# Eight probability tiles, one mixing per batch element, reciprocals in the bank of the mixed values, and a new order on every queue

## The chip, the cores and the metric
The kernel runs on one core of a Trainium2 chip. The metric is the device time of one execution in microseconds, the median of several runs. TensorE is called PE, VectorE the vector engine or DVE, ScalarE ACT, GpSimd POOL and SyncE SP, as in the profile.

## What is computed
A batch of 64 sequences of 128 tokens with 256 channels goes through two blocks of attention and feed-forward, each on a layer-normalised input with a residual added:

```python
x = x + L0_xattn(_layernorm(x), ctx, ctx, mask, ...)   # 16 heads of 16 channels, biases
x = x + L0_ffn(_layernorm(x), W1, b1, W2, b2)          # ternary weights, 1024 hidden, relu
x = x + L1_xattn(_layernorm(x), ctx, ctx, lens, ...)   # keys beyond lens masked
x = x + L1_ffn(_layernorm(x), ...)                     # 8 autoencoders, the best one's adapter
```

Both attentions are `softmax(q k^T / 4) v` per head and take keys and values from the same context. The last layer computes for each sequence the reconstruction error of eight small autoencoders, picks the best, and adds a base matmul and that expert's adapter.

## The kernel before
**Pairs and slots.** The batch is cut into 32 pairs of sequences (`NP`, `PB` = 2, so `T` = 256 tokens). One loop `for t in range(FIRST, END)` is written out for each engine. `at(t, o)` yields pair p where `t = 16 p + o`, so a step with offset o runs for pair p in slot 16 p + o, and offsets 0 to 77 mean that up to five pairs are in work at once. Within a slot the order is that of the text. A slot is no unit of time: it only fixes the order of instructions on each engine's own queue. Across engines everything is ordered by semaphores (`Signal`).

**Attention of one layer l for a pair.** `scores(l, p, j)`, j = 0 to 7 (four for each sequence b), puts four heads' scores of 128 x 128 into the bank `S`; `maximum(l, p, j)` on the vector engine takes the row maxima (layer 0 adds the mask's bias, line 863; layer 1, line 855). After four of them `split_max(l, p, b)` splits the 16 maxima of each token into two half-precision parts and turns them into rows (`mrows`, lines 870 to 877). SP's `maxima(l, p, b)` copies these rows with four transfers into `qs`, as two more rows of the contraction. `scores_t(l, p, j)` then computes the transposed scores with the maximum already taken off into the bank `X`, `exps` on ACT turns them into a tile of `pT`, and in layer 0 POOL's `apply_mask` multiplies the tile by the mask. `mix(l, p, u)` multiplies two such tiles with the values into half of the bank `V`: 8 matmuls with 32 columns of weights each, four side by side in the array. Half of a head's 32 columns of weights hold ones, so that the softmax's denominator comes with the values. `turn_out(l, p, b)` transposes `V` in 32 x 32 blocks to `otok`, `scale_out(l, p, b)` takes the reciprocals (`rden`), multiplies (`atok`) and transposes to `attT`, and `output(l, p)` projects. `add_att` adds the result, `statistics` computes the moments of the next layer norm.

**Keys and queries.** `keys` and `queries` leave their result in a bank; `high` (ACT) and `low` (vector engine) split it into two half-precision parts in `packed`; SP's `spill(l, j, p)` (j = 1 keys, 0 queries) writes that to DRAM and `stack(l, j, p)` reads it back head by head with four transfers (and one for the mask's row of the keys). `scores(l, p, 0)` waits for all nine transfers of the two stacks.

**The last layer.** `hidden`, `reconstruct(p, m)` (experts 2m and 2m + 1, row groups of 64), `differences(p, e)` on the vector engine, `squares` on ACT, `losses`, `choose`, SP's `gather` of the chosen adapter (two transfers of 192.5 KB), `down`, `up`, `add_up`, `store`.

**Banks.** `S`, `X` and `V` are one bank each; all other results share five banks dealt out in `BANKS`. `claim` makes PE wait until the former holder of a bank has been read. `exps(l, p, j)` writes tile `j % 4` of four and waits for the mixing that read it.

**SP's order** within a period: `maxima(1, 1)`, `load`, `stack(1, 1)`, `spill(1, 0)`, `maxima(0, 0)`, `stack(1, 0)`, `gather`, `spill(0, 1)`, `maxima(0, 1)`, `stack(0, 1)`, `spill(0, 0)`, `maxima(1, 0)`, `stack(0, 0)`, `store`, `spill(1, 1)`.

Of the kernel before, what the change touches and what calls it, by code (L numbers as in the profile page):

```python
# [8 lines left out]
F32 = mybir.dt.float32  # L9
# [13 lines left out]
H = 16  # L23
# [10 lines left out]
UNITS = 2 * PB  # L34
# [13 lines left out]
def pair16(value):  # L48
# [14 lines left out]
END = BODY * (NP - 1) + 77  # L63
# [34 lines left out]
def build(nc, x, lens, mask, mask_t, wq0, bq0, wk0, bk0, wv0, bv0, wo0, bo0, w1t, b1, w2t, b2,  # L98
          wq1, wk1, wv1, wo1, w_base, wd1, bd1, wd2, bd2, adapters, ctx_in, out):
    with ExitStack() as ctx:  # L100
# [118 lines left out]
        mix_ready = [signal(f"mix_ready{l}", UNITS) for l in range(2)]  # L219
# [101 lines left out]
        def _(sp):  # L321
# [84 lines left out]
            for t in range(FIRST, END):  # L406
                for p in at(t, 48):
                    maxima(1, p, 1)
                for p in at(t, -14):
                    load(p)  # L410
                for p in at(t, 34):
                    stack(1, 1, p)
                    spill(1, 0, p)
                for p in at(t, 4):
                    maxima(0, p, 0)
                for p in at(t, 36):
                    stack(1, 0, p)
                for p in at(t, 71):
                    gather(p)
                for p in at(t, -7):  # L420
                    spill(0, 1, p)
                for p in at(t, 10):
                    maxima(0, p, 1)
                for p in at(t, -6):
                    stack(0, 1, p)
                for p in at(t, -5):
                    spill(0, 0, p)
                for p in at(t, 44):
                    maxima(1, p, 0)
                for p in at(t, -4):  # L430
                    stack(0, 0, p)
                for p in at(t, 76):
                    store(p)
                for p in at(t, 29):
                    spill(1, 1, p)
# [9 lines left out]
        def _(pool):  # L445
# [73 lines left out]
            def apply_mask(p, j):  # L519
                exp_done[0].done(pool, p, j)  # L520
                keep_ready.done(pool, p)
                blk = pT[:, j % 4].rearrange("p (a t) -> p a t", a=4)
# [8 lines left out]
            for t in range(FIRST, END):  # L531
                for p in at(t, 16):
                    normalise(1, p, 0)
                for p in at(t, 19):
                    normalise(1, p, 1)
                for p in at(t, -11):
                    mask_parts(p)
                    rstd_of(0, p)
                for p in at(t, -10):
                    normalise(0, p, 0)  # L540
                    normalise(0, p, 1)
                for p in at(t, 6):
                    apply_mask(p, 0)
                for p in at(t, 7):
                    apply_mask(p, 1)
                for p in at(t, 23):
                    h_lows(p, 0)
                for p in at(t, -8):
                    mask_bias(p)
                for p in at(t, 8):  # L550
                    apply_mask(p, 2)
                for p in at(t, 24):
                    h_lows(p, 1)
                for p in at(t, 9):
                    apply_mask(p, 3)
                for p in at(t, 26):
                    add_bias(1, p)
                for p in at(t, -6):
                    add_bias(0, p)
                for p in at(t, 26):  # L560
                    h_lows(p, 2)
                    h_lows(p, 3)
                for p in at(t, 10):
                    apply_mask(p, 4)
                for p in at(t, 58):
                    rstd_of(3, p)
# [3 lines left out]
                for p in at(t, 11):  # L570
                    apply_mask(p, 5)
                for p in at(t, 12):
                    apply_mask(p, 6)
                for p in at(t, 13):
                    apply_mask(p, 7)
                for p in at(t, 29):
                    rstd_of(2, p)
                    normalise(2, p, 0)
                for p in at(t, 30):
                    normalise(2, p, 1)  # L580
                for p in at(t, 15):
                    rstd_of(1, p)
# [7 lines left out]
        def _(act):  # L590
# [32 lines left out]
            def exps(l, p, j):  # L623
                st_ready[l].done(act, p, j)
                if j >= 4:
# [842 lines left out]
```

## Time and profile before
| | |
|---|---|
| median of 3 runs | 1717.36 us (1717.09 to 1728.58) |
| the profiled execution | 1727.22 us, span 1725.2 us |
| mean granted TensorE clock | 0.969 of full speed |
| PE busy | 1584.5 us, 92%, 15136 matmuls |
| vector engine busy | 1316.8 us, 76% |
| ACT busy | 891.8 us, 52% |
| POOL busy | 1104.2 us, 64% |
| DMA | 157.24 MB, 91 GB/s |

The span runs from the first to the last instruction of one execution; the rest of its time lies around it. Busy time is the union of an engine's instructions; a PE matmul's length contains the tail of its pipeline, so the distance from one start to the next is the better measure of what a block costs. An idle time is listed with the event that ended it. The chain that ended last goes back from the last instruction to what released each step.

### The profile page before, as it was taken

To read this page: it belongs to the slowest core of one execution; us is meant where nothing else is said; L and a number is where in the kernel's file an instruction comes from. 1 tells how busy PE (TensorE), PEld (TensorE's weight loads), DVE (VectorE), ACT (ScalarE), POOL (GpSimd) and SP (SyncE) were. 2 spreads that over 40 slices of the span, in tenths; PEclk is the share of its full clock that TensorE was granted. 3 is DMA by queue.
4 is the path that set the end of the run, shared out by engine and by line. 5 is a ranking of instruction groups with operands and counts; after the bars stand their busy time and mean duration, and the time that the engine had idled before them with its cause. 6 is when DMAs were issued, how large, how long until landed. Compare 5 with 4: busy or idle time off the path is not lost.

```text
span 1725.2 us, 44058 instructions
## 1 busy us (share of the span) xinstructions
PE 1584.5 (92%) x15136; PEld 1279.1 (74%) x15136; DVE 1316.8 (76%) x5086; ACT 891.8 (52%) x2465; POOL 1104.2 (64%) x1198
## 2 busy tenths in 40 slices
PE   2578999999999999999999999999999999999776
PEld 1356777778878887778887877788788877877554
DVE  6446788888887888888887888888788888886542
ACT  0134455655555556555555556555555565555432
POOL 4467776666676776666667766666677766655200
PEclk9789999999999999999999999999999999999976
DMA  7445555555555454555555545555555555552300
GB/s 187 81 74 92 87 88 92 96 103 97 97 95 108 83 96 96 103 97 94 97 103 94 94 90 98 101 95 99 97 106 82 97 97 102 97 77 54 57 18 26
DMA packets 286213, 157.24 MB, mean 91 GB/s; under 512 B 38820, under 2 KB 281640, under 8 KB 285992
## 3 DMA queue, kind: packets, MB, share of 16 engines
q1 hardware_dynamic: 285992, 154.44, 49.6%
q8 instruction: 121, 1.98, 0.6%
q14 instruction: 100, 0.82, 0.2%
HBM read 111.36 MB, written 41.96 MB: 89 GB/s over the span
## 4 chain that ended last, share of the span: by engine, by line
PE 47%; DVE 38%; issue 7%; DMA 3%; POOL 2%; ACT 1%; SPq 1%; DVEq 0%; ACTq 0%; POOLq 0%
DVE dump L863 11%; PE psD L1239 7%; PE psD L1228 7%; DVE dif L929 6%; PE psD L1207 4%; PE psD L1153 4%; PE psD L1273 4%; PE psS L1168 3%; PE psD L1142 3%; PE psV L1195 3%; PE psX L1180 3%; DVE atok L894 3%; PE psD L1249 3%; DVE otok L886 2%; DVE m L872 2%
## 5 line engine op out<-in xcount | busy, mean ns | idle before, releaser
L633 ACT ACTIVATE pT<-psX 128x512 f32<-128x512 f32 x512 | 305.9, 597 | 351.7 <-PE psX L1180 351.6
L523 POOL TENSOR_TENSOR pT<-pT,keep 128x512 f32<-128x512 f32 x256 | 323.1, 1268 | 108.2 <-ACT pT L633 105.6
L508 POOL TENSOR_SCALAR xn<-xr,mv,rstd 128x256 f32<-128x256 f32 x256 | 311.5, 1224 | 13.7
L855 DVE TENSOR_REDUCE mx<-psS 128x4 f32<-128x512 f32 x256 | 175.7, 686 | 170.8 <-PE psS L1168 168.4
L482 POOL TENSOR_SCALAR veps<-mv 128x2 f32<-128x2 f32 x128 | 29.5, 230 | 392.3 <-DVE mv L808 389.6
L929 DVE SCALAR_TENSOR_TENSOR dif<-psD,bd2s,xT 128x256 f32<-128x256 f32 x512 | 216.8, 472 | 63.6 <-PE psD L1249 63.5
L863 DVE CUSTOM_DVE_ANT_0 dump<-psS,bias 128x128 bf16<-128x128 f32 x1024 | 232.5, 282 | 30.8 <-PE psS L1168 30.7
L1168 PE MATMUL psS<-ks,qs 65*128 65x128 f16 x2048 | 202.6, 221 | 49.2 <-DVE mx L863 22.6
L677 ACT ACTIVATE dif<-dif 128x256 f32<-128x256 f32 x512 | 207.4, 412 | 25.8 <-DVE dif L929 24.7
L1180 PE MATMUL psX<-qs,ks 67*128 67x128 f16 x2048 | 200.4, 220 | 15.5 <-ACT pT L633 8.7
L1168 PEld LDWEIGHTS psS<-ks,qs 65*128 65x128 f16 x2048 | 141.6, 98 | 97.8 <-issue 34.0
L1180 PEld LDWEIGHTS psX<-qs,ks 67*128 67x128 f16 x2048 | 141.6, 98 | 55.6 <-issue 18.6
L1195 PE MATMUL psV<-pT,v 128*32 128x128 f32 x4096 | 165.9, 280 | 8.0 <-POOL pT L523 4.3
L528 POOL TENSOR_TENSOR hhl<-work,hhl 128x512 f16<-128x512 f32 x128 | 151.5, 1193 | 11.9 <-ACT hhl L663 11.9
L1207 PE MATMUL psD<-wo,attT 128*128 128x256 f32 x512 | 132.1, 403 | 19.3 <-DVE attT L898 19.2
L1249 PE MATMUL psD<-hd,wd2s 64*128 64x256 f32 x1024 | 146.3, 405 | 2.0 <-DVE dif L929 2.0
L1195 PEld LDWEIGHTS psV<-pT,v 128*32 128x32 f32 x4096 | 96.8, 109 | 61.4 <-issue 39.3
L1220 PE MATMUL psD<-xs,w1q 128*128 128x256 f16 x1024 | 134.0, 274 | 1.4 <-DVE xs L911 0.8
L1142 PE MATMUL psD<-xT,wq 128*128 128x256 f32 x512 | 132.0, 394 | 1.5 <-DVE keep L822 1.5
L1153 PE MATMUL psD<-wv,ctxT 128*128 128x256 f32 x512 | 130.5, 399 | 0.0
L606 ACT ACTIVATE xT<-psD 128x512 f32<-128x512 f32 x96 | 57.1, 595 | 137.4 <-PE psD L1113 137.4
L1239 PE MATMUL psD<-xT,wd1s 128*128 128x256 f32 x512 | 126.0, 390 | 0.7 <-ACT xT L606 0.7
(103 smaller groups left out, 3125.3 us busy)
## 6 DMA issues: line engine op xcount, KB each, us to landing
scr<-packed SPq DMA_DIRECT2D x128, 256.0 KB, 2.3
ks<-scr SPq DMA_DIRECT2D x256, 128.0 KB, 4.5
qs<-scr SPq DMA_DIRECT2D x256, 128.0 KB, 4.4
adapter<-in_adapters SPq DMA_DIRECT2D x64, 192.5 KB, 2.5
xr<-in_x SPq DMA_DIRECT2D x32, 256.0 KB, 2.8
ctxT<-in_ctx SPq DMA_DIRECT2D x32, 256.0 KB, 2.8
qs<-mrows SPq DMA_DIRECT2D x512, 2.0 KB
out_y<-xr SPq DMA_DIRECT2D x32, 256.0 KB, 4.9
```

The costliest lines, as they stand in the source:

```text
L508: nc.gpsimd.tensor_scalar(xn[:, XN[s], b], xr[:, p % NX, b], mv[:, s, b, 0:1], rstd[:, s, b:b + 1], ALU.subtract, ALU.mult).then_inc(norme ...
L523: nc.gpsimd.tensor_tensor(blk, blk, keep[:, p % 2, j // 4].unsqueeze(1).to_broadcast([P, 4, P]), ALU.mult).then_inc(masked.sem, 1)
L633: nc.scalar.activation(pT[:, j % 4], X[:], ACT.Exp, scale=SCALE).then_inc(exp_done[l].sem, 1)
L677: nc.scalar.activation(blk, blk, ACT.Square, accum_out=acc[:, e, b:b + 1]).then_inc(squared.sem, 1)
L863: ins = nc.vector.tensor_tensor_reduce(out=dump[:, a], in0=S[:, a * P:a * P + P], in1=bias0[:, p % 2, b], scale=1.0, scalar=-3e38, op0=ALU ...
L929: nc.vector.scalar_tensor_tensor(out=dif[:, e % 4, k], in0=bank[f"rec{e}"][:, k * T:k * T + T], scalar=bd2s[:, e, k:k + 1], in1=xT3[:, p % ...
L1153: ins = nc.tensor.matmul(dst[:, b * D:b * D + D], ctxT[:, p % NC, k * T + b * P:k * T + b * P + P], wv[l][:, k], start=(k == 0), stop=(k = ...
L1168: ins = nc.tensor.matmul(S[:, a * P:a * P + P], qs[0:MASK_ROW + 1, r, h, t0:t0 + P], ks[0:MASK_ROW + 1, r, h, t0:t0 + P], start=True, stop ...
L1180: ins = nc.tensor.matmul(X[:, a * P:a * P + P], ks[0:ROWS, r, h, t0:t0 + P], qs[0:ROWS, r, h, t0:t0 + P], start=True, stop=True)
L1195: ins = nc.tensor.matmul(V[32 * a:32 * a + 32, (2 * half + s) * P:(2 * half + s) * P + P], v2[l][:, b, half * UH + 2 * a + s], pT[:, (2 * ...
L1207: ins = nc.tensor.matmul(dst[:, b * D:b * D + D], attT[:, l, b, k], wo[l][:, k], start=(k == 0), stop=(k == KD - 1))
L1239: ins = nc.tensor.matmul(dst[:, m * T:m * T + T], wd1s[:, k, e0:e0 + 2].rearrange("p e r -> p (e r)"), xT3[:, p % 2, k], start=(k == 0), s ...
```

## The change
`pT` has eight tiles instead of four, so that `exps` writes tile j and waits only for the other layer's mixing of a neighbouring pair. `mix(l, p, b)` does all four tiles of a sequence in one go and signals once. It claims `V` after `normalised` (the multiplication) instead of `turned`, since the reciprocals now lie in `V[:, 0:H]` and no longer in `rden`. The five banks are dealt anew. And every queue has a new order. The sum of the work is the same.

```diff
-    ("cnt", "rec5", "v1", "hd0", "q0"),
-    ("v0", "q1", "T2", "F1_1", "T0", "hd1", "T3"),
-    ("O0", "F1_2", "rec1", "loss", "rec7", "up"),
-    ("O1", "k0", "rec6", "rec3", "F2", "down", "rec0"),
-    ("rec2", "F1_0", "T1", "k1", "F1_3", "rec4"),
+    ("F1_0", "q1", "O0", "F1_3", "T0", "rec1", "F1_1", "hd0", "up"),
+    ("v0", "rec4", "rec3", "k1", "hd1", "down", "T3"),
+    ("loss", "rec7", "rec0", "F1_2"),
+    ("k0", "rec6", "T2", "v1", "O1"),
+    ("rec2", "cnt", "T1", "rec5", "F2", "q0"),
...
-        pT = sb("pT", [P, 4, 512], F32)
+        pT = sb("pT", [P, QUADS, 512], F32)
-        rden = sb("rden", [P, 2, H], F32)
...
             def exps(l, p, j):
                 st_ready[l].done(act, p, j)
-                if j >= 4:
-                    mix_ready[l].done(act, p, (j - 4) // 2)
-                elif l:
-                    mix_ready[0].done(act, min(p + 2, NP - 1), 2 + j // 2)
-                    mix_ready[1].done(act, p - 1, 2 + j // 2)
+                if l:
+                    mix_ready[0].done(act, min(p + 2, NP - 1), j // 4)
                 else:
-                    mix_ready[1].done(act, p - 3, 2 + j // 2)
-                    mix_ready[0].done(act, p - 1, 2 + j // 2)
-                nc.scalar.activation(pT[:, j % 4], X[:], ACT.Exp, scale=SCALE).then_inc(exp_done[l].sem, 1)
+                    mix_ready[1].done(act, p - 3, j // 4)
+                nc.scalar.activation(pT[:, j], X[:], ACT.Exp, scale=SCALE).then_inc(exp_done[l].sem, 1)
...
             def turn_out(l, p, b):
-                mix_ready[l].done(dve, p, 2 * b + 1)
+                mix_ready[l].done(dve, p, b)
...
-                nc.vector.reciprocal(rden[:, l], otok[:, l, :, HD]).then_inc(recip_done[l].sem, 1)
+                nc.vector.reciprocal(V[:, 0:H], otok[:, l, :, HD]).then_inc(recip_done[l].sem, 1)
                 recip_done[l].done(dve, p, b)
-                nc.vector.tensor_tensor(atok[:, l], otok[:, l, :, 0:HD], rden[:, l].unsqueeze(2).to_broadcast([P, H, HD]),
+                nc.vector.tensor_tensor(atok[:, l], otok[:, l, :, 0:HD], V[:, 0:H].unsqueeze(2).to_broadcast([P, H, HD]),
...
-            def mix(l, p, u):
-                b, half = u // 2, u % 2
-                if half == 0:
-                    claim("V", turned[l], p, b)
-                if u == 0:
+            def mix(l, p, b):
+                claim("V", normalised[l], p, b)
+                if b == 0:
...
-                (exp_done[1] if l else masked).done(pe, p, 2 * u + 1)
-                for s in range(2):
+                (exp_done[1] if l else masked).done(pe, p, 4 * b + 3)
+                for n in range(4):
                     for a in range(4):
...
```

The new orders, cut to the period of 16 slots as they follow one another in the loop. Numbers in brackets are the slot within the period; steps of different pairs stand side by side.

SP: [2] `store`, [3] `maxima(1, 1)`, [5] `load`, [6] `spill(1, 0)`, [7] `maxima(0, 0)`, `stack(1, 0)`, [8] `gather`, [9] `maxima(0, 1)`, [10] `spill(0, 1)`, [12] `spill(1, 1)`, `stack(0, 1)`, [13] `spill(0, 0)`, `maxima(1, 0)`, `stack(0, 0)`, `stack(1, 1)`.

PE: [0] `reconstruct(1)`, `scores(0, 0)`, `scores_t(1, 2)`, [1] `values(1)`, `scores(0, 1)`, `scores_t(1, 3)`, `output(0)`, `turn(2)`, [2] `scores(0, 2)`, `mix(1, 0)`, `scores_t(1, 4)`, `reconstruct(2)`, [3] `scores_t(1, 5)`, `scores(0, 3)`, [4] `queries(1)`, `reconstruct(3)`, `scores(0, 4)`, `turn(1)`, `scores_t(1, 6)`, [5] `values(0)`, `scores_t(1, 7)`, `scores(0, 5)`, `keys(0)`, `count`, [6] `ffn_up(0)`, `losses`, `scores(0, 6)`, `scores_t(0, 0)`, `mix(1, 1)`, [7] `scores(0, 7)`, `scores_t(0, 1)`, [8] `ffn_up(1)`, `keys(1)`, `scores_t(0, 2)`, `turn(0)`, `scores(1, 0)`, [9] `ffn_up(2)`, `scores_t(0, 3)`, `scores(1, 1)`, [10] `ffn_up(3)`, `output(1)`, `scores_t(0, 4)`, `scores(1, 2)`, [11] `queries(0)`, `scores_t(0, 5)`, `scores(1, 3)`, [12] `down`, `scores_t(0, 6)`, `scores(1, 4)`, `mix(0, 0)`, `up`, [13] `scores_t(0, 7)`, `scores(1, 5)`, `ffn_down(0)`, `turn(3)`, [14] `ffn_down(1)`, `scores(1, 6)`, `hidden(0)`, `hidden(1)`, `scores_t(1, 0)`, [15] `scores(1, 7)`, `reconstruct(0)`, `scores_t(1, 1)`, `mix(0, 1)`.

The vector engine's first half, old: [0] `differences(1)`, `maximum(0, 0)`, `scale_out(0, 1)`, [1] `differences(2)`, `maximum(0, 1)`, `differences(3)`, `add_att(0)`, [2] `maximum(0, 2)`, `statistics(1)`, `turn_out(1, 0)`, [3] `maximum(0, 3)`, `differences(4)`, `differences(5)`, [4] **`split_max(0, 0)`**, `low(1, 0)`, `statistics(0)`, `differences(6)`, `maximum(0, 4)`, `any_of`, [5] `differences(7)`, `x_lows`, and so on. New: [0] `differences(1)`, `split_max(1, 1)`, `turn_out(0, 1)`, `maximum(0, 0)`, [1] `scale_out(0, 1)`, `differences(2)`, `maximum(0, 1)`, `differences(3)`, [2] `add_att(0)`, `maximum(0, 2)`, `statistics(1)`, `turn_out(1, 0)`, [3] `differences(4)`, `differences(5)`, `maximum(0, 3)`, `statistics(0)`, [4] `low(1, 0)`, `maximum(0, 4)`, `differences(6)`, `any_of`, **`split_max(0, 0)`**, `differences(7)`, `x_lows`, [5] `maximum(0, 5)`, [6] `scale_out(1, 0)`, `maximum(0, 6)`, `choose`, `values0`, and so on; the period ends in both with [15] `maximum(1, 7)` and `differences(0)`, which in the old order had `statistics(2)`, `split_max(1, 1)` and `turn_out(0, 1)` around them.

On POOL the layer norm's steps and `add_bias` move by up to four slots among the eight `apply_mask`; on ACT `squares`, `values1`, the `high` and `h_highs` steps move by one or two.

## Rows read from the trace of the kernel before
**Rows 1.** The stage table: window, us, busy times (instructions), clock, DMA share, GB/s.
```profile
400.00:600.00 200.00, 195.93 (x1922) 160.10 (x1922) 163.82 (x641) 112.43 (x312) 140.53 (x154) 1.00 0.55 98
```

**Rows 2.** The page: PE's busy tenths in 40 slices.
```profile
PE   2578999999999999999999999999999999999776
```

**Rows 3.** PE's waits, 400 to 1400 us: total, times, longest.
```profile
PE psD L1207 <- DVE attT L898: 10.2, 20, 0.5
PE psS L1168 <- DVE mx L863: 8.2, 20, 0.5
```

**Rows 4.** The chain that ended last, in order of time: start, us, what.
```profile
848.46 0.29 DVE dump L863
...
873.91 0.46 DVE attT L898
...
897.40 0.29 DVE dump L863
```

**Rows 5.** PE's timeline: start, us, line, output and input, shapes, count.
```profile
853.44 0.65 PE L1195 MATMUL psV<-pT,v 128*32 128x128 f32 x16
854.01 1.14 PE L1249 MATMUL psD<-hd,wd2s 64*128 64x256 f32 x8
...
870.12 0.39 PE L1168 MATMUL psS<-ks,qs 65*128 65x128 f16 x4
...
893.51 1.14 PE L1249 MATMUL psD<-hd,wd2s 64*128 64x256 f32 x8
894.57 0.65 PE L1195 MATMUL psV<-pT,v 128*32 128x128 f32 x16
...
896.98 0.39 PE L1168 MATMUL psS<-ks,qs 65*128 65x128 f16 x4
897.20 0.39 PE L1180 MATMUL psX<-qs,ks 67*128 67x128 f16 x4
897.52 0.70 PE L1249 MATMUL psD<-hd,wd2s 64*128 64x256 f32 x4
```

**Rows 6.** The mixing's line, weight loads: ns min/median/max, first and last start.
```profile
L1195 PEld LDWEIGHTS psV<-pT,v x2624: 106/110/110, 405.1 to 1397.1; 128*32 128x32 f32 x188
```

**Rows 7.** The vector engine's timeline, columns as in rows 5.
```profile
856.61 1.66 DVE L929 SCALAR_TENSOR_TENSOR dif<-psD,bd2s,xT 128x256 f32<-128x256 f32 x4
858.18 0.17 DVE L870 TENSOR_SCALAR m<-mx 128x16 f16<-128x16 f32 x1
...
858.72 0.65 DVE L837 TENSOR_TENSOR packed<-psD,packed 128x512 f16<-128x512 f32 x1
...
862.11 0.87 DVE L929 SCALAR_TENSOR_TENSOR dif<-psD,bd2s,xT 128x256 f32<-128x256 f32 x2
...
867.67 0.75 DVE L886 STREAM_TRANSPOSE otok<-psV 128x256 f32<-128x256 f32 x2
...
869.57 1.08 DVE L872 SCALAR_TENSOR_TENSOR m<-mx,m 128x16 f16<-128x16 f32 x1
```

**Rows 8.** SP's timeline: start and length of issues, their count.
```profile
886.25 3.31 SPq L361 DMA_DIRECT2D qs<-scr  x4
...
957.74 2.61 SPq L377 DMA_DIRECT2D qs<-mrows  x4
960.39 1.88 SPq L361 DMA_DIRECT2D qs<-scr  x4
```

**Rows 9.** The tile `qs`, 961.7 to 962.4 us: its stack's last transfers.
```profile
DMA to landing us min/median/max: 4.8/4.9/5.1
```

**Rows 10.** Two lines of the vector engine: ns min/median/max.
```profile
L894 DVE TENSOR_TENSOR atok<-otok,rden x81: 424/425/830, 409.1 to 1387.9; 128x256 f32<-128x256 f32 x81
...
L845 DVE TENSOR_TENSOR v<-psD,bvb x40: 411/417/424, 423.8 to 1354.1; 128x256 f32<-128x256 f32 x40
```

**Rows 11.** POOL's timeline, columns as in rows 5.
```profile
869.47 1.15 POOL L528 TENSOR_TENSOR hhl<-work,hhl 128x512 f16<-128x512 f32 x1
```

More of the change, by code:

```diff
@@ L693, in _ @@
                 for p in at(t, 49):
+                    values1(p)
                     exps(1, p, 3)
@@ L729, in _ @@
                     h_highs(p, 0)
+                for p in at(t, -9):
+                    high(0, 1, p)
+                for p in at(t, 23):
                     relus(p, 1)
+                for p in at(t, 8):
+                    exps(0, p, 2)
+                for p in at(t, -8):
+                    copy_xT(0, p)
                 for p in at(t, 24):
                     high(1, 1, p)
-                for p in at(t, 8):
-                    exps(0, p, 2)
                 for p in at(t, 25):
@@ L974, in _ @@
                     differences(p, 1)
+                for p in at(t, 48):
+                    split_max(1, p, 1)
+                for p in at(t, 16):
+                    turn_out(0, p, 1)
                 for p in at(t, 0):
                     maximum(0, p, 0)
-                for p in at(t, 16):
+                for p in at(t, 17):
                     scale_out(0, p, 1)
@@ L992, in _ @@
                     turn_out(1, p, 0)
-                for p in at(t, 3):
-                    maximum(0, p, 3)
                 for p in at(t, 67):
@@ L997, in _ @@
                     differences(p, 5)
+                for p in at(t, 3):
+                    maximum(0, p, 3)
+                for p in at(t, -13):
+                    statistics(0, p)
+                for p in at(t, 36):
+                    low(1, 0, p)
+                for p in at(t, 4):
+                    maximum(0, p, 4)
+                for p in at(t, 68):
+                    differences(p, 6)
+                for p in at(t, -12):
+                    any_of(p)
                 for p in at(t, 4):
                     split_max(0, p, 0)
[L1000 to L1003 removed]
                 for p in at(t, 68):
[L1005 to L1010 removed]
                     differences(p, 7)
[L1012 removed]
+                for p in at(t, 20):
                     x_lows(p)
@@ L1023, in _ @@
                     choose(p)
-                for p in at(t, 54):
-                    turn_out(1, p, 1)
+                for p in at(t, 6):
+                    values0(p)
                 for p in at(t, 7):
@@ L1069, in _ @@
                     maximum(1, p, 7)
-                    split_max(1, p, 1)
                 for p in at(t, 63):
                     differences(p, 0)
-                for p in at(t, 15):
-                    turn_out(0, p, 1)
                 if t == GAMMA_SLOT:
@@ L1282, in _ @@
             for t in range(FIRST, END):
-                for p in at(t, 48):
-                    values(1, p)
+                for p in at(t, 64):
+                    reconstruct(p, 1)
                 for p in at(t, 0):
@@ L1327, in _ @@
                     scores_t(1, p, 7)
-                for p in at(t, -11):
-                    count(p)
                 for p in at(t, 5):
@@ L1333, in _ @@
                     keys(0, p)
+                    count(p)
                 for p in at(t, 22):
                     ffn_up(p, 0)
+                for p in at(t, 70):
+                    losses(p)
                 for p in at(t, 6):
@@ L1350, in _ @@
                     scores_t(0, p, 2)
+                for p in at(t, -8):
+                    turn(0, p)
                 for p in at(t, 40):
@@ L1379, in _ @@
                     scores(1, p, 3)
-                for p in at(t, 75):
-                    up(p)
+                for p in at(t, 76):
+                    down(p)
+                for p in at(t, 12):
+                    scores_t(0, p, 6)
                 for p in at(t, 44):
```

258 lines of the change are left out of this document (115 added, 143 removed).

## The prediction

> **What bounds the kernel now.** I read the stage table first, then PE's waits, the chain of waits, and last the timelines of one period. In the loop PE is busy 195.93 of 200 us, the vector engine 163.82, ACT 112.43, POOL 140.53, at a granted clock of 1.00 [rows 1]. About 28 periods of a pair run so: the slices with a 9 for PE [rows 2] are some 1,380 us. A period is 48.94 us (the chain's row at 848.46 comes back at 897.40). Only 1 us a period is idle: 10.2 us before the output projection in 20 periods and 8.2 us before `scores` [rows 3]. An idle time begins when the last matmul's 0.39 us are over, though the next could have followed after 0.22 (the row at 896.98 [rows 5]), so 0.17 is lost ahead of each: 0.51 + 0.17 and 0.41 + 0.17, 1.26 us in all.
>
> The chain says where the period is made. From the first maximum (848.46) to the transposed `attT` (873.91) it runs without a break on the vector engine, then on PE to the next `scores(0, p, 0)` [rows 4]. So the first half is bound by the vector queue in order, the second by PE. Work put into the first vector half lengthens the period, unless something there has slack.
>
> I count from R, the end of `reconstruct(p, 0)`: 893.51 + 1.06 = 894.57 [rows 5], one period earlier 845.63. Layer 1's `scores(1, p, 0)` starts at 870.12, R + 24.49, and from there PE needs 24.45 us to the next R.
>
> **What PE saves.** A mixing unit starts at 853.44 and the next block at 854.01: 0.57 us. It has four rounds of four column groups, and a round's weight loads take 110 ns each [rows 6]; if rounds follow at that spacing they are 0.44, and 0.13 is paid once per unit (between 0 and that; I take it whole, since 0.57 is not a multiple of the spacing), and 8 units become 4: 4 x 0.13 = 0.53 us. Before a unit or a `reconstruct`, the full-array block in front takes 0.10 more: 896.98 to 897.20 is 0.22 for a score block, 897.20 to 897.52 is 0.32 [rows 5]. There are 8 such entries in the old order, 7 in the new one: 0.10. PE's work is thus 0.63 lighter. Without the 1.26 of waiting a period would be 48.94 - 1.26 - 0.63 = 47.05 us. (The Trainium skill, TensorEngine Tiling (Array Packing), Key Properties, says that changing the tiling mode drains the engine; by it alone each of the five boundaries that go would pay, and the rows agree with 0.10 to 0.13 at each.)
>
> **What the vector engine pays.** The new order puts five steps ahead of `split_max(0, p, 0)` that followed it: `low(1, 0)`, `statistics(0)`, `differences(6)`, `maximum(0, p, 4)`, `any_of`. They are one unbroken stretch in the old trace: 858.72 to 862.11, 3.39 us [rows 7]. What stood ahead of it stays: 848.46 to 858.18, 9.72 us. The split itself is 858.72 - 858.18 = 0.54, and its last instruction ends some 0.08 after the next one's start: 0.62. From the first maximum, M, the rows of layer 0 are now ready at M + 9.72 + 3.39 + 0.62 = M + 13.73.
> M: the old one was R + 2.83, set by `scores(0, p, 0)`. Now the queue in front is four difference instructions (856.61 to 858.18, 1.57), `split_max(1, p, 1)`, 0.54, and `turn_out(0, p, 1)`, 0.75 less the overlap of some 0.07 [rows 7], from R + 0.12: M = R + 2.91. PE reaches its score block at 0.33 of `scores_t` + mixing 1.01 + `reconstruct` 1.06 = R + 2.40 as before, so neither waits for the other. Rows ready: R + 16.64.
>
> **Where that goes: SyncE.** SP's queue is in order: spill of the queries of layer 1 (its low part is ready at about R + 14.2, well ahead), `maxima(0, p, 0)`, then `stack(1, 0, p)`. The stack cannot be issued before the maxima, and the maxima not before the rows. Issue of the four row transfers takes 957.74 to 960.39, 2.65 us, and the stack's last transfer is issued at 960.39 + 1.88 - 0.45 = 961.82 and lands 5.1 later: 6.5 us from the stack's first issue to its last landing [rows 8, 9]. So the stack lands at R + 16.64 + 0.1 + 2.65 + 6.5 = R + 25.9, and `scores(1, p, 0)` starts at R + 26.0. In the old order it came at 24.49 with no row of waiting.
> PE would be there earlier. Its blocks from R to this one were 24.49 less the wait of 0.58; new among them are `scores_t(1, p, 1)` 0.23, `turn(0)` 0.44, one unit more in fewer pieces, 0.57 - 3 x 0.13 = 0.18, and one entry 0.10: 24.86. So 1.1 us of waiting is in it. A part of it may be spent earlier, at `scores_t(0, p, 0)`, which wants the same rows in `qs` at R + 19.8 when their last transfer is issued at about R + 18.7; no row gives their landing, and up to 1.1 it costs nothing extra.
> After it PE has less left than before: 24.45, less three units and their entries (3 x 0.57 + 3 x 0.10), less `scores_t(1, p, 1)` 0.23 and `turn(0)` 0.44 which moved ahead, less the old wait 0.68, less 0.05 of a slower transpose behind a unit, plus one merged mixing and its entry, 1.11: 22.15. Period: 26.0 + 22.15 = **48.15**, and I take 48.2 for small waits that such a sum overlooks (ACT's exponential 5 behind `high(0, 0)`, and the bank of `turn(0)` freed by `relus` at nearly the moment it is wanted).
>
> **The rest of the change.** Eight tiles for the probabilities take away waits of ACT for a mixing; `exps` waits for `scores_t` in the old profile, so that is worth 0. The price is that a mixing waits for four masks: POOL ends mask 3 some 2 us ahead of PE. Hidden by that slack. Held `V`: the bank is now free after the multiplication, not after the transpose, under 1 us later, and each mixing comes at least that much after `scale_out`: 0.
> Reciprocals in PSUM: `atok` takes 424 ns mostly and 830 at worst [rows 10]; the long one starts while POOL works on a two-input instruction. The same is seen at 869.57, where an instruction of 16 elements took 1.08 us (one of 858.18 took 0.17), to the end of POOL's 869.47 + 1.15 [rows 7, 11]. With one operand in PSUM I expect no holds: 0.4 of 4 x 0.45 us a period, but at `scale_out(1, 1)`, which no longer sets PE's time. A vector instruction of 256 elements with a PSUM operand takes 417 ns [rows 10], so 0 for the place, between -0.4 and +0.1.
> (Here a rule speaks against: the Trainium skill, VectorE: DVE Perf Modes, section on the TRN2 errata, gives PSUM sources 62 cycles more than SBUF ones; by it the one `scale_out` on the chain would add under 0.1 us a period. The rows, 417 against 424, do not show it.)
> Banks are dealt anew: I followed each claim; the closest, `count` behind `x_lows`, costs under 0.1. The stores move behind five slots in SP's order, past `gather` and `load`, which are issued long before their data is wanted.
>
> **The sum.** 48.94 - 48.2 = 0.74 us a period x 28 = 21 us. Filling and draining the loop I charge with 1 us more, for mixings that wait for four tiles. The profiled execution: 1725.2 - 20 = 1705 of span. It was 1727.22 us where the median of the runs is 1717.36, so the forecast is 1717.4 - 20 = **1697 us**.
>
> **Rivals.**
> *A, the stack is not late.* Then PE alone bounds: 47.05, say 47.1. 28 x 1.84 = 52 us: 1666. For it: PE idles only 1 us now. Against: six terms from rows make the chain 1.1 us longer than PE's blocks ahead of it. Chance 0.10.
> *B, no change.* The chain is a little longer than I add up: the stack's issue can stall (886.25 took 3.31 us for four such transfers [rows 8], 1.4 more than 960.39), or a short vector instruction is held 0.9 us behind POOL as at 869.57, now in the split of layer 0. A stall or a hold adds 0.5 to 0.9: 48.7 to 49.1, 1711 to 1722. POOL has no two-input mask work at that time, which speaks against the hold. Chance 0.30.
> *C, slower: `gather` shares the DMA engines with the late stack.* SP can issue it once `choose` is done on the vector engine, by the same counting at R + 21.6, so in the middle of the stack's flight; the old order had it as the stack landed. If they divide the engines' time, up to 2.5 us come on top: period 50.7, + 1.76 x 28 = 49 us: 1767. It decides from 1.35 us on (slower by 1%). For it: the engines carry other traffic in half of the time already (DMA share 0.55 [rows 1]). Against: the transfers are on one queue, the stack's first, and its issue is over at about R + 21.4. Chance 0.17, with other new waits of that size.
> *The forecast*: chance 0.43, by itself 1685 to 1708.
>
> About 1% is what a measurement of this kernel can tell from no change. Faster by over 1% (below 1700): A and most of the forecast, 0.47. Within 1%: the rest of the forecast and B, 0.34. Slower: 0.19 (C and a little of B). Range: 1668 to 1735, which leaves out half of A and two thirds of C.
>
> **What would show it.** Right: a period near 48.2; a wait of PE of about 1 us at `scores(1, p, 0)` for the transfer into `qs`, perhaps one at `scores_t(0, p, 0)` for the rows, none before the output projection; merged mixings of 1.01 us; `atok` never over 450 ns. Wrong: no DMA among PE's waits (A); a stack landing 8 us or more after its issue (C); waits of PE for POOL's masks or for the vector engine's `scale_out`, which would mean that the slack of the merged mixing was misread.

## The result

| | changed kernel | kernel before |
|---|---|---|
| median of the runs, same chip | 1709.21 us (1706.53 to 1712.03, 7 runs) | 1719.5 us (1717.09 to 1728.58, 7 runs) |
| ratio | 0.992, 95% interval 0.9899 to 0.9941 | |
| profiled execution | 1706.53 us | 1727.22 us |
| its span | 1704.7 us | 1725.2 us |

Faster by 0.8%. The forecast of the span was 1705 us, that of the time 1697. The measured 1709.21 lies in the stated range, and 1 us above the 1685 to 1708 that the forecast gave for its own case. Span and time differ so much because the sum was made against the profiled execution, and taken off the median. The profiled execution of before lay 8 us above the median of its runs, that of the changed kernel 3 us below. The same instructions in the same order were timed once more on another chip (the run with the gather later, below): 1710.51 us against 1724.23, ratio 0.9918.

### The profile after

The stage table of the loop's first stretch, which answers to [rows 1] (columns as there):

```profile
400.00:600.00 200.00, 194.98 (x1967) 162.13 (x1965) 159.63 (x653) 118.15 (x321) 138.62 (x150) 1.00 0.60 97
```

PE is no busier than before. Its waits between 400 and 1400 us, which answer to [rows 3] (columns: waited for; us in total, times, longest us):

```profile
PE psS L1165 <- DMA qs<-scr: 13.8, 21, 1.1
PE psX L1177 <- DMA qs<-mrows: 10.2, 21, 0.6
```

The two old waits are gone: none before the output projection, next to none for `mx`. In their place stand two for SP's transfers, in every period: at `scores_t(0, p, 0)` for the rows of maxima, and at `scores(1, p, 0)` for the stack of layer 1. One period on PE (start, duration, what is computed, and in brackets the wait ahead of it); R, the end of `reconstruct(p, 0)`, is 838.40, where `scores_t(1, p, 1)` begins, and the last row is the next one's:

```profile
838.40 0.40 PE L1177 MATMUL psX<-qs,ks 67*128 67x128 f16 x4
838.73 1.08 PE L1190 MATMUL psV<-pT,v 128*32 128x128 f32 x32
839.74 1.13 PE L1244 MATMUL psD<-hd,wd2s 64*128 64x256 f32 x8
...
858.83 0.38 PE L1177 MATMUL psX<-qs,ks 67*128 67x128 f16 x4 [0.46 <-DMA qs<-mrows]
...
864.88 0.38 PE L1165 MATMUL psS<-ks,qs 65*128 65x128 f16 x4 [0.78 <-DMA qs<-scr]
...
866.20 0.39 PE L1165 MATMUL psS<-ks,qs 65*128 65x128 f16 x4
...
886.89 0.40 PE L1177 MATMUL psX<-qs,ks 67*128 67x128 f16 x4
```

A merged mixing takes 839.74 - 838.73 = 1.01 us, `scores(1, p, 0)` begins at R + 26.48, and the next R is 22.01 later (886.89). Over 22 periods the two are 26.36 and 22.06 on average: 48.42 us. (In all that follows, places in a period are averages over the 21 to 23 periods that begin between 400 and 1450 us, unless one is shown.) The same chain on the vector engine and on SP (SP's rows: start of the first issue, time of issuing, transfers):

```profile
851.86 0.66 DVE L832 TENSOR_TENSOR packed<-psD,packed 128x512 f16<-128x512 f32 x1
...
854.06 0.41 DVE L809 TENSOR_REDUCE allc<-mqf 128x2 f32<-128x256 f32 x1
854.38 0.17 DVE L865 TENSOR_SCALAR m<-mx 128x16 f16<-128x16 f32 x1
854.59 0.18 DVE L867 SCALAR_TENSOR_TENSOR m<-mx,m 128x16 f16<-128x16 f32 x1
854.80 0.21 DVE L872 STREAM_TRANSPOSE mrows<-m 128x32 f16<-128x32 f16 x1
...
855.04 2.59 SPq L375 DMA_DIRECT2D qs<-mrows  x4
857.67 1.88 SPq L359 DMA_DIRECT2D qs<-scr  x4
860.97 1.53 SPq L383 DMA_DIRECT2D adapter<-in_adapters  x2
```

Rows ready at 855.01, R + 16.6; stack issued from 857.67, R + 19.3; landed when PE goes on, 7.2 us later (7.09 on average: 6.95 to the last landing, and then the start of the block). The period, from one `add_up` to the next, is 48.95 us before (26 intervals, all within 0.1) and 48.37 after (47.6 to 49.0: it moves with the landings). Of the 20.5 us between the spans, 14.9 are these 26 intervals, 0.6 came before the first, and 5.0 lie in the last five.

**What else is gone.** The old order had two more losses on the vector engine, in each of 22 periods, and both stood on the chain that ended in the projection of `attT`. The split of layer 0's second batch, `split_max(0, p, 1)`, was held for 0.9 us behind POOL ([rows 7] has one, at 869.57), and the multiplication ahead of that projection took 0.64 to 0.83 us instead of 0.42:

```profile
873.05 0.82 DVE L894 TENSOR_TENSOR atok<-otok,rden 128x256 f32<-128x256 f32 x1
```

In the changed kernel the first is held in 3 of 22 periods and the second in none. What the old kernel would gain if only these two were taken away was not tried.

### The profile page after: what moved, and what is told of

The parts are those of the page before. It is cut to its first block, busy times and chain, and to the rows that moved or that the text cites. A ratio compares the mean times of both kernels' runs of the same rounds, so it can differ in the third digit from the quotient of the medians.

```text
span 1704.7 us, 43831 instructions
## 1 busy us (share of the span) xinstructions
PE 1554.4 (91%) x15136; PEld 1282.7 (75%) x15136; DVE 1271.5 (75%) x5086; ACT 912.5 (54%) x2465; POOL 1098.4 (64%) x1198
## 4 chain that ended last, share of the span: by engine, by line
PE 45%; DVE 24%; DMA 12%; issue 9%; SPq 7%; POOL 2%; ACT 1%; POOLq 0%; DVEq 0%; ACTq 0%
DMA qs<-scr 10%; DVE dif L924 7%; DVE dump L858 7%; PE psD L1234 6%; PE psD L1223 6%; SPq L375 4%; PE psS L1165 4%; PE psD L1202 4%; PE psD L1139 4%; PE psD L1268 3%; PE psD L1215 3%; PE psX L1177 3%; PE psD L1244 3%; SPq L359 2%; PE psV L1190 2%
## 5 line engine op out<-in xcount | busy, mean ns | idle before, releaser
L522 POOL TENSOR_TENSOR pT<-pT,keep 128x512 f32<-128x512 f32 x256 | 318.6, 1271 | 5.5 <-ACT pT L629 5.5
L1165 PEld LDWEIGHTS psS<-ks,qs 65*128 65x128 f16 x2048 | 136.8, 98 | 114.9 <-issue 70.6
L653 ACT ACTIVATE work<-psD,b1s 128x256 f32<-128x256 f32 x256 | 107.8, 475 | 71.2 <-PE psD L1215 60.1
L1190 PE MATMUL psV<-pT,v 128*32 128x128 f32 x4096 | 140.1, 278 | 5.2 <-POOL pT L522 3.4
L1127 PE MATMUL psD<-ctxT,wk 128*128 128x256 f32 x512 | 124.6, 387 | 13.3 <-DVE bqr L961 13.3
L1223 PE MATMUL psD<-w2q,hhl 128*128 128x256 f16 x1024 | 122.0, 273 | 0.5 <-POOL hhl L527 0.5
```

Of the source, the lines that this page charges most:

```text
L522: nc.gpsimd.tensor_tensor(blk, blk, keep[:, p % 2, j // 4].unsqueeze(1).to_broadcast([P, 4, P]), ALU.mult).then_inc(masked.sem, 1)
L1165: ins = nc.tensor.matmul(S[:, a * P:a * P + P], qs[0:MASK_ROW + 1, r, h, t0:t0 + P], ks[0:MASK_ROW + 1, r, h, t0:t0 + P], start=True, stop ...
L1223: ins = nc.tensor.matmul(dst[:, b * D:b * D + D], hhl[:, n % 2, n // 2, b * P:b * P + P], w2q[:, n // 2], start=(n == 0), stop=(n == 2 * K ...
```

## The experiments

The ratios are to the kernel before on the same chip. "Period" is the mean of the same 26 intervals, and the changed kernel's is 48.37.

### The chain, from both sides

**The split early, in the changed kernel.** `split_max(0, p, 0)` goes ahead of the five steps:

```
                 for p in at(t, 3):
                     maximum(0, p, 3)
+                    split_max(0, p, 0)
...
-                for p in at(t, 4):
-                    split_max(0, p, 0)
```

> The changed kernel with split_max(0, p, 0) moved on the vector engine from behind any_of to right behind maximum(0, p, 3), where the old order had it in effect; nothing else. My theory: the rows of layer 0 come about 3.4 us earlier, SP can issue them as soon as the spill of layer 1's queries is out (about R + 15.2 instead of R + 16.6), the stack lands near R + 24.9 and PE hardly waits for it: period 47.4 instead of 48.4 us, in all about 25 us less than the changed kernel, 1683 us, and PE's waits for the transfers into qs nearly gone. Rival (PE's work alone made the gain, the transfer waits are only where its slack happens to fall): the waits move elsewhere, less than 5 us of difference.

Measured: 1757.67 us, ratio 1.0182 (1.0165 to 1.0199), period 50.41. The transfers are hardly waited for any more, as the chain says: `scores(1, p, 0)` starts at R + 24.91 in most periods, where the forecast had PE ready at R + 24.86. But the kernel lost 2%. Its waits of PE:

```profile
PE psS L1164 <- DVE mx L850: 36.3, 20, 2.0
PE psS L1164 <- DMA qs<-scr: 2.0, 3, 1.0
```

and what stands behind the first of them, vector engine and POOL, then PE:

```profile
839.03 0.62 DVE L865 TENSOR_SCALAR m<-mx 128x16 f16<-128x16 f32 x1
839.68 1.20 DVE L867 SCALAR_TENSOR_TENSOR m<-mx,m 128x16 f16<-128x16 f32 x1
...
838.46 1.16 POOL L527 TENSOR_TENSOR hhl<-work,hhl 128x512 f16<-128x512 f32 x1 [0.23 <-ACT hhl L659]
839.58 1.27 POOL L514 TENSOR_TENSOR xr<-xr,bob 128x512 f32<-128x512 f32 x1
...
843.86 0.40 PE L1164 MATMUL psS<-ks,qs 65*128 65x128 f16 x4 [1.66 <-DVE mx L850]
...
845.05 3.42 PE L1201 MATMUL psD<-wo,attT 128*128 128x256 f32 x8
```

The other split, that of the second batch, now falls among POOL's two-input instructions. Its two instructions of 16 elements end with POOL's (839.65 with 839.62, 840.88 with 840.85) and take 1.82 us instead of 0.35 (2.2 in most periods). PE waits 1.66 us at `scores(1, p, 1)`, and then its granted clock falls. The table of that run has, for the 5 us before and the 3.4 us behind,

```profile
840.00:845.00 5.00, 3.34 (x37) 2.79 (x35) 4.90 (x13) 3.91 (x8) 4.85 (x5) 1.00 0.24 68
845.40:848.80 3.40, 3.40 (x13) 2.56 (x12) 0.97 (x3) 0.61 (x2) 2.76 (x3) 0.50 0.76 187
```

0.50 is the lower of the two levels, 1.2 instead of 2.4 GHz, so the output projection takes 3.42 us instead of 1.95. All 21 periods between 400 and 1450 us have the hold, but only 15 of them the lower clock. The length of the one wait doesn't tell which: behind a longer one the clock stayed, behind a shorter one, in another period, it fell:

```profile
894.76 0.40 PE L1164 MATMUL psS<-ks,qs 65*128 65x128 f16 x4 [1.99 <-DVE mx L850]
895.00:900.00 5.00, 5.00 (x36) 4.17 (x34) 3.99 (x10) 1.44 (x3) 3.89 (x4) 1.00 0.70 167
...
1193.34 0.45 PE L1164 MATMUL psS<-ks,qs 65*128 65x128 f16 x4 [1.09 <-DVE mx L850]
1193.60:1197.00 3.40, 3.40 (x16) 2.56 (x14) 1.92 (x4) 1.66 (x4) 3.40 (x3) 0.50 0.55 162
```

The 6 periods at full clock last 49.22 us, the 15 others 50.82. The hold alone thus costs 1.7 us a period against the 47.55 of the run below that has the early split without it, and the clock 1.6 more where it falls.

**The split late, in the kernel before**, behind `any_of`:

```
-                for p in at(t, 4):
-                    split_max(0, p, 0)
...
                 for p in at(t, -12):
                     any_of(p)
+                for p in at(t, 4):
+                    split_max(0, p, 0)
```

> The kernel before, with only split_max(0, p, 0) moved behind any_of on the vector engine, as the changed order has it. Theory of the chain: the rows come 3.4 us later, the stack of layer 1's queries lands at about R + 25.9, PE waits 1.5 us for it at scores(1, p, 0) and in exchange no longer for attT (0.7): period 49.7 instead of 48.94, about 21 us slower than before, 1740 us. Rival (PE and the vector engine bound the kernel, the transfers are hidden): within 3 us of the kernel before.

Measured: 1751.78 us, ratio 1.0143 (1.0122 to 1.0165), period 50.11. PE's waits show the two transfers of the changed kernel, and none for `attT`:

```profile
PE psS L1168 <- DMA qs<-scr: 26.4, 20, 1.9
PE psX L1180 <- DMA qs<-mrows: 14.8, 20, 0.9
```

So the wait for the stack follows the place of this one step, in either kernel. It is the price that the new slots pay. The period is 0.4 us longer than was expected, and the trace has the 0.4 in the stack's flight: it is issued from R + 19.3, as in the changed kernel, and `scores(1, p, 0)` starts at R + 26.3, 7.0 us later, where 25.9 was expected. From there to the next R it is 23.7, as expected.

### The two other parts

**Reciprocals in SBUF.**

```
+        rden = sb("rden", [P, 2, H], F32)
...
-                nc.vector.reciprocal(V[:, 0:H], otok[:, l, :, HD])...
-                nc.vector.tensor_tensor(atok[:, l], otok[:, l, :, 0:HD], V[:, 0:H].unsqueeze(2)...
+                nc.vector.reciprocal(rden[:, l], otok[:, l, :, HD])...
+                nc.vector.tensor_tensor(atok[:, l], otok[:, l, :, 0:HD], rden[:, l].unsqueeze(2)...
```

> The changed kernel with the reciprocals back in SBUF (rden), all else as changed. Theory of the holds: atok takes up to 0.83 us again when POOL has a two-input instruction in work, and one of the four in a period (scale_out(1, 1)) stands right ahead of the output projection of layer 1, where PE has no slack: about 0.3 us a period, 9 us in all, 1718 us. Rival (the place of 16 numbers does not matter, as I took it in the sum): 0, within 2 us of the changed kernel. By the rule on PSUM sources it would be faster by 1 to 2 us.

Measured: 1724.5 us, ratio 0.9993 (0.998 to 1.0005), period 49.02: 0.65 more, twice what was expected. The group of the multiplication in this kernel and in the changed one, 400 to 1400 us (busy us, mean ns | idle before):

```profile
L890 DVE TENSOR_TENSOR atok<-otok,rden 128x256 f32<-128x256 f32 x81 | 47.7, 589 | 2.8
```

```profile
L889 DVE TENSOR_TENSOR atok<-otok,psV 128x256 f32<-128x256 f32 x83 | 34.9, 421 | 2.9
```

and the place in this kernel's timeline where it matters (POOL, vector engine, PE):

```profile
872.82 2.49 POOL L523 TENSOR_TENSOR pT<-pT,keep 128x512 f32<-128x512 f32 x2
...
874.57 1.02 DVE L890 TENSOR_TENSOR atok<-otok,rden 128x256 f32<-128x256 f32 x1
...
876.22 1.97 PE L1203 MATMUL psD<-wo,attT 128*128 128x256 f32 x8 [0.37 <-DVE attT L894]
```

With both inputs in SBUF it is held behind POOL's two-input masks, in `scale_out(1, p, 1)`, and PE waits for it at `output(1, p)`, 5.4 us in 13 periods between 400 and 1400 us. From `scores(1, p, 0)` to the next R a period takes 22.51 us instead of 22.06, so 0.45 of the 0.65 can be put down to this place. The rest lies ahead of it, where the stack's landing varies, and no cause is shown. With one input in PSUM no instance is held. In the changed kernel `attT` is done at 867.10 and the projection begins at 867.30: a slack of 0.20.

**Mixings in halves**, each with its own entry, one score block apart (shown for one of the four):

```
+                for p in at(t, 50):
+                    mix(1, p, 0, 0)
                 for p in at(t, 2):
                     scores(0, p, 2)
                 for p in at(t, 50):
-                    mix(1, p, 0)
+                    mix(1, p, 0, 1)
```

> The changed kernel with each mixing issued in two halves again, with the score block that stood in front of it between them; still one signal, and V and the tiles as changed. PE's work grows by 4 x (0.13 + 0.10) = 0.9 us a period. Theory (the period is set by the chain over SP, whose wait absorbs what PE does ahead of it): three of the four mixings lie ahead of scores(1, p, 0) in a stretch with about 1.1 us of waiting, so only mix(0, 0) counts: 0.25 a period, about 7 us in all, 1716 us, and the wait for the stack shrinks by 0.7. Rival (PE bound): 0.9 a period, 26 us, 1735 us.

Measured: 1742.58 us, ratio 1.0095 (1.0073 to 1.0117), period 49.54, above both numbers. One split mixing:

```profile
844.37 0.39 PE L1177 MATMUL psX<-qs,ks 67*128 67x128 f16 x4
844.69 0.64 PE L1191 MATMUL psV<-pT,v 128*32 128x128 f32 x16
845.27 0.40 PE L1165 MATMUL psS<-ks,qs 65*128 65x128 f16 x4
845.59 0.65 PE L1191 MATMUL psV<-pT,v 128*32 128x128 f32 x16
846.17 1.13 PE L1270 MATMUL psD<-wb,xT 128*128 128x256 f32 x4
```

Two halves of 0.58 and two entries of 0.10 are 1.36, where the merged one has 1.01 + 0.10: 0.25 each, 1.0 us a period, near the 0.92 of the terms. The expectations went wrong on what a chain does with it. After `scores(1, p, 0)`, where PE bounds, 0.24 of it shows in most periods (22.24 against 22.00), the one mixing that stands there, and 0.37 on average (22.43 against 22.06). Ahead of it half a mixing now stands before `scores(0, p, 2)`, which the vector queue waits for in order (11.1 us in 20 periods, none in the changed kernel): that score block comes at R + 8.1 instead of R + 7.3, the rows at R + 17.4 instead of 16.6, and `scores(1, p, 0)` at R + 27.17 instead of 26.36. Of these 0.8 us, 0.14 come from the split mixing at R, and some 0.65 from the half that this edit puts ahead of the block, with its entry, where the merged mixing stands behind it. So the run prices this way of halving. It doesn't show that merging as such shortens the vector chain.

### Toward a version without the waits

**Three runs that were not what they were meant to be.** In this kernel the slots decide the order: a step of slot `o` is placed by `o` modulo 16, and the place in the text only orders steps of one slot. In the next three runs the edit on POOL (twice) and the one on SP moved text, and not slots.

```
 (POOL, with the split early as above)
-                    mask_bias(p)
                     normalise(0, p, 0)
...
                 for p in at(t, -9):
                     add_bias(0, p)
+                for p in at(t, -11):
+                    mask_bias(p)
+                for p in at(t, 22):
+                    h_lows(p, 0)
```

> The changed kernel with split_max(0, p, 0) right behind maximum(0, p, 3), as in the run with the early split, and with one more edit on POOL: mask_bias (two one-input instructions, 1.54 us) moves from ahead of normalise(0, p, 0) to behind add_bias(0, p), and h_lows(p, 0) behind it. The two-input add_bias(0) is then over about 1.1 us before split_max(0, p, 1), and h_lows(0) begins about when it ends, so only the one-input instruction is in flight. If the early split lost its gain to that hold (theory): split_max(0, p, 1) takes 0.54 us again instead of 1.9, no wait of 1.7 to 2.0 us at scores(1, p, 1), no fall of the clock, no DMA among PE's longer waits: period 47.3 to 47.7, 28 x 0.9 = 25 us under the changed kernel, ratio to before 0.977, about 1685. If the early split makes the vector queue itself too late for scores(1, p, 1) (rival): period 48.4 or more, ratio 0.992 or more.

As built, `mask_bias` moved behind `normalise(0, p, 0)` only, and `h_lows(p, 0)` stayed ahead of `add_bias(0, p)`. Measured: 1756.36 us, ratio 1.0205 (1.0177 to 1.0233), as the early split alone, with 35.8 us of waits for `mx` in 20 periods against 36.3. It says nothing on the theory.

> The changed kernel with split_max(0, p, 0) two steps earlier only (ahead of differences(6) and any_of, 1.11 us of vector work), and the same POOL edit as the run before it. The chain to the stack of layer 1 is 1.11 us shorter: the waits for the rows at scores_t(0, p, 0) (0.46 in the profile) and for the stack at scores(1, p, 0) (0.78) leave about 0.1 together: period 48.43 - 1.0 = 47.4 to 47.6, ratio 0.978, about 1687. Rival, the landing times set the rest and spread: a wait of 0.3 to 0.5 stays and the period is 47.9, ratio 0.985.

The split is moved as told (ahead of `differences(6)`), the POOL edit is the same ineffective one. Measured: 1747.08 us, ratio 1.0141 (1.011 to 1.0173), waits for `mx` 33.1 us, for the transfers 2.3. So even 1.1 us of an earlier split brings the collision: what shields the second split in the changed kernel is PE's wait of 0.46 us at `scores_t(0, p, 0)`, which delays POOL's `h_lows` behind it: the second split starts at R + 23.2 in the changed kernel and in this one, and POOL's instruction at R + 23.6 there and R + 23.0 here. (The lower clock follows in 10 of 21 periods; these last 50.8 us, nearly all others 49.2.) And the shield is thin. In the changed kernel's own trace POOL's instruction starts at 862.01, 0.02 after the split's second one ends, and 3 of 22 periods show the hold (at 813.52, 1.06 us instead of 0.18).

> The changed kernel with gather(p) behind maxima(0, p, 1) in the order of SP, so that the 2 adapters are not on the queue while the stack of layer 1 is in flight. Theory (no sharing worth speaking of): the stack lands as before, 7 us behind its first issue, period within 0.1 of 48.43, ratio 0.992. Rival (the adapters share the engines with the stack): it lands 0.5 us or more earlier, PE's waits for it fall by 10 us of 21 in 20 periods, period 47.9, ratio 0.983. Slower by up to 0.3 a period if the queue of SP, 1.5 us later behind it, makes a spill late.

Here SP's order came out unchanged, so this is the changed kernel timed again: 1710.51 us, ratio 0.9918 (0.9892 to 0.9944), period 48.43.

The kernel before was profiled once more as well.

> The kernel before once more, for a second profile: the profiled execution shown was 1727.22 us where the median is 1717.36. If the 10 us lie in the loop, its period is 48.6 here against 48.94 there; if they lie at the start or the end, the period is 48.94 again and the first add_up comes earlier than 248.1 us, or the last one's tail is shorter.

Measured: 1727.68 us, period 48.94 again; the first `add_up` at 251.3 us (248.1 in the other), the last five intervals 198.5 us (201.1). In both the loop is the same and the ends differ by 3 us, in opposite directions. Both profiled executions lie at the upper end of this kernel's runs (1717 to 1729), so where the 10 us down to its median lie stays open.

**The POOL edit in slots that work.**

```
                 for p in at(t, -11):
-                    mask_bias(p)
                     normalise(0, p, 0)
...
                 for p in at(t, 22):
                     add_bias(1, p)
-                    h_lows(p, 0)
                 for p in at(t, -9):
                     add_bias(0, p)
+                    mask_bias(p)
+                for p in at(t, 23):
+                    h_lows(p, 0)
```

> The edit that the two runs before were meant to have, now in the slots that put it there: on POOL, add_bias(0, p) directly behind add_bias(1, p), then mask_bias(p) (one input, 1.54 us), then h_lows(p, 0); with split_max(0, p, 0) behind maximum(0, p, 3) as in the run with the early split. Counted from R of that run: add_bias(0) ends at R + 22.4, mask_bias fills R + 22.4 to 23.9, and split_max(0, p, 1) runs at R + 23.56 to 24.1. Theory (the hold by POOL's two-input instructions ate the gain of the early split): no hold, scores(1, p, 0) at R + 25.2, the vector queue lets scores(1, p, 1) start at R + 26.9, from there 20.7 to the next R as in the changed kernel: period 47.6, 28 x 0.8 = 23 us under the changed kernel, ratio 0.979, about 1687. Rival (the vector queue is late there even without a hold, or the hold only moves): period 48.4 or more, ratio 0.992 or more.

Measured: **1680.93 us** (1676.78 to 1684.1), ratio 0.9733 (0.9713 to 0.9753), period 47.55: faster than both kernels. POOL, then the vector engine, in the period whose R is 829.39:

```profile
850.47 1.28 POOL L514 TENSOR_TENSOR xr<-xr,bob 128x512 f32<-128x512 f32 x1
851.85 1.52 POOL L475 TENSOR_SCALAR bias<-mqf,allc 128x128 f32<-128x128 f32 x2
853.45 1.17 POOL L527 TENSOR_TENSOR hhl<-work,hhl 128x512 f16<-128x512 f32 x1
...
852.60 0.17 DVE L866 TENSOR_SCALAR m<-mx 128x16 f16<-128x16 f32 x1
852.80 0.24 DVE L868 SCALAR_TENSOR_TENSOR m<-mx,m 128x16 f16<-128x16 f32 x1
```

The split lies inside POOL's one-input instructions and takes 0.44 us. The second instruction's 0.24 instead of 0.18 is all that is left of the hold. `scores(1, p, 0)` comes at R + 24.91, `scores(1, p, 1)` at R + 26.64. What PE still waits for, and the stage table's first row:

```profile
PE psS L1165 <- DVE mx L851: 3.9, 17, 0.3
PE psS L1165 <- DMA qs<-scr: 1.7, 2, 1.3
```

```profile
400.00:600.00 200.00, 199.08 (x2025) 165.66 (x2023) 163.68 (x675) 120.75 (x332) 138.39 (x150) 1.00 0.61 100
```

PE is now the bound but for one place. The period is 0.5 us above the 47.05 that the forecast reckoned for PE's work alone, and 0.4 of it is, in 17 periods between 400 and 1400 us, the wait for `mx` at `scores(1, p, 1)`: 0.23 as listed, and the 0.17 that is lost ahead of each wait.

> The changed kernel with that POOL edit alone. In its trace split_max(0, p, 1) runs just ahead of POOL's two-input h_lows(0) and is not held, so there is nothing to gain: period 48.4, ratio 0.992. If POOL's new order makes something late (h_lows(0) by 0.5 us, the masks by nothing), up to 0.3 a period more, ratio 0.997.

Measured: 1708.9 us, ratio 0.9894 (0.9877 to 0.9912), period 48.45. The POOL edit alone brings nothing and costs nothing, and the early split alone costs 2%. Together they bring 1.6 to 1.9% on the changed kernel.

**The adapters behind the stack.**

```
-                for p in at(t, 72):
-                    gather(p)
                 for p in at(t, 9):
                     maxima(0, p, 1)
+                for p in at(t, 73):
+                    gather(p)
```

> The changed kernel with gather(p) issued behind maxima(0, p, 1) on SP, this time in the slot that puts it there (the run with the gather later had the changed kernel's order unchanged): the two adapters are off the queue while the stack of layer 1 is in flight. Theory (no sharing worth speaking of): the stack still lands 7 us behind its first issue, period within 0.1 of 48.43, ratio 0.992. Rival (they share the engines with it): it lands 0.5 us or more earlier, PE's waits for it fall from 14 us in 21 periods to under 5, period 47.9, ratio 0.982. If the later queue of SP makes a spill late, slower by 0.1 to 0.3 a period.

Measured: 1701.75 us, ratio 0.986 (0.9842 to 0.9878), period 48.27. Its waits:

```profile
PE psX L1177 <- DMA qs<-mrows: 10.1, 21, 0.6
PE psS L1165 <- DMA qs<-scr: 8.9, 20, 1.5
PE psD L1259 <- DMA adapter<-in_adapters: 1.7, 2, 0.9
```

The time from the stack's first issue to PE going on is 6.89 us on average over 21 periods (6.55 to 8.0), 7.09 in the changed kernel (6.60 to 7.55), and the waits fall from 13.8 to 8.9 us. Two other traces with the adapters ahead, the changed kernel timed again and the run with the POOL edit alone, have 7.17 and 7.15. So the adapters do take something from the stack, 0.2 to 0.3 us: between the two expectations. Twice PE now waits for an adapter, and the period is only 0.1 shorter.

## Why the forecast came out as it did

**The chain: right.** First half bound by the vector queue, then SP, then a landing. Rows ready at R + 16.6 (forecast 16.64), the stack issued from R + 19.3 (19.39), waits at the two blocks that were named and none before `output(1)`. Without the stack's wait PE comes to `scores(1, p, 0)` at R + 24.91 (24.86). Both kernels with that one step moved confirm the cause.

**The stack's flight: mis-sized.** The sum had 6.5 us from first issue to landing, and 0.1 until PE goes on; here it is 6.95 and 0.14. With an issue 0.12 earlier this puts `scores(1, p, 0)` at R + 26.36 and not 26.0. The 6.5 was one transfer's 5.1 from the old trace; the average there, over 22 periods, is 6.6 (6.3 to 7.4), so 0.1 of the gap is a single transfer taken for the average. Another 0.2 to 0.3 is rival C, the adapters on the same engines: real, at a tenth of the price that the rival gave it (2.5 us). That it is so little because the stack's issue is over before the adapters' is likely and not shown. The landing varies by 1 us in a chain in which nothing absorbs it.

**After it: right.** 22.15 by the sum, 22.0 in 20 of 22 periods. In the two longer ones (22.5 and 22.7) the second batch's split was held, and a third hold cost nothing: rival B's mechanism is there, but in the other batch's split, and rare. Period 48.2 forecast, 48.37 measured, and so 15 us of the loop instead of 19 in these 26 intervals. (The 28 periods come from the slices with a 9, which are 33 and some 1,420 us, not 1,380: 29 periods, 0.7 us in the sum.)

**The ends: luck.** 1 us was charged for mixings that wait for four tiles, and the ends gave 5.6 us back, 5.0 of it in the last five intervals (196.1 against 201.1). That made up what the loop lacked, and the forecast of the span is as close as it is for this reason. It is not a property of the change: in the second profiles of the two kernels the last five differ by 0.3 (198.2 and 198.5) and the spans by 16.4, and the run with the POOL edit alone has 201.0.

**Reciprocals in PSUM: taken as 0, which does not hold.** The failed step is the clause that `scale_out(1, 1)` no longer sets PE's time. It has 0.2 us of slack ahead of the output projection, and a hold of up to 0.6 us goes through it. Taken back, the edit costs 0.65 us a period and 0.7% of the time: nearly the whole gain, of which 0.45 is traced to that place. My sum had no holds in it, so its total did not suffer. That the old kernel's vector chain had 1.3 us of such holds (0.9 in a split and mostly 0.4 in the multiplication), and that the new one has almost none, the prediction didn't follow up.

**Merged mixings: right in size** (1.01 us; 1.0 a period for taking it back on PE, against 0.92). What the halves cost beyond that comes from where they were put.

**From the span to the median: wrong.** 20 us less than a profiled execution that stood 10 above the median was taken off the median. The medians differ by 10 to 14 us on two chips.

**Rival A** (1666 us) needed the stack not to be late. With the step and POOL moved that state is reached: 1681.

## What to carry to other kernels

When one step in an in-order queue is moved, follow it through every queue behind it (here the vector engine, SP, the landing, PE) and give the landing its spread, not its best value. A change that removes a wait shifts all engines against each other: look at what the wait kept apart, since here 0.46 us of waiting kept two 16-element instructions clear of a hold that, with the lower clock behind it, cost 2.9 us a period (50.41 against 47.55). An edit that should be neutral, as where 16 reciprocals lie, is worth its own run. Compare a profiled execution with a profiled execution, and a median with a median.

## What the runs showed of the hardware

- An instruction of 16 elements on the vector engine, reading and writing SBUF, took 0.62 to 1.20 us instead of 0.17 while POOL ran instructions with two SBUF inputs, ending with them; during POOL's one-input `mask_bias` it took 0.17 and 0.24. The 256-element multiplication with two inputs in SBUF took 589 ns on average and up to 1293, with one of them in PSUM 421 and never more than 423. (The Trainium skill, SBUF — State Buffer, section on the two separate sides of SBUF, has the two engines share one pair of ports, so that a vector instruction with two SBUF inputs and a GpSimd instruction that reads SBUF exclude each other. The traces agree where POOL has two inputs. Where POOL has one, as `mask_bias`, which reads SBUF and ran to 853.37, they don't: the vector instruction with two SBUF inputs was over at 853.04.)
- In the run with the early split the granted clock fell to 0.50 behind PE's wait in 15 of 21 periods, and an output projection took 3.42 us instead of 1.95. It fell behind a wait of 1.09 us and stayed at 1.00 behind one of 1.99, and with the late split in the old kernel 20 of 21 periods, with waits of 0.9 to 1.9 us, kept 1.00.
- Four transfers of 128 KB took 6.6 to 7.5 us from the first issue until PE went on behind the last landing, in one and the same loop.
